# Three slots of an attention block's step reordered on TensorE, and a weight load moved forward in the load queue

## What is computed

```python
q = proj(query, Wk, bk); k = proj(key, Wk, bk); v = proj(values, Wv, bv)
scores = einsum("bhqd,bhkd->bhqk", q, k) / sqrt(dk)
p = softmax(where(allow, scores, NEG))
left = sum(p) - cumsum(p)
effect = clip(exp(-softplus(gamma) * sqrt(clip(left * |i - j|, 0))), 1e-5, 1e5)
attn = softmax(where(allow, scores * effect, NEG))
out = einsum("bhqk,bhkd->bhqd", attn, v)
x = layer_norm(query + concat(out) @ Wo.T + bo)
x = layer_norm(x + relu(x @ W1.T + b1) @ W2.T + b2)
```

## Time and profile before

| | us |
|---|---|
| median of 3 runs | 1475.06 |
| lowest and highest of the 3 runs | 1474.28, 1477.92 |
| the profiled execution, its own time | 1475.0 |
| span of that execution in the trace, first to last instruction | 1473.2 |
| TensorE busy | 1420.9 (96%) |
| VectorE busy | 1083.1 (74%) |
| ScalarE busy | 1026.9 (70%) |
| mean granted TensorE clock | 0.990 |

### The profile page before, as it was taken

How to read it: one execution, slowest core, us unless ns; L and a number is a source line. 1 busy time by engine, 2 the same in 40 slices (tenths; PEclk the granted TensorE clock), 3 DMA queues, 4 the chain that set the end, 5 groups by cost and what they waited for, 6 DMA issues and landing times.

```text
span 1473.2 us, 32758 instructions
## 1 busy us (share of the span) xinstructions
PE 1420.9 (96%) x12140; PEld 1154.5 (78%) x12140; DVE 1083.1 (74%) x3780; ACT 1026.9 (70%) x2626; POOL 155.2 (11%) x180
## 2 busy tenths in 40 slices
PE   5798899999999999999999999999999999999998
PEld 4455688888888888888888888888888888888787
DVE  6997868787887767786777868767786776777433
ACT  4775768777777768776677777668676776777522
POOL 4212010101001010000001010000100101000100
PEclk9999999999999999999999999999999999999999
DMA  8766667667576656656665655566656666666975
GB/s 286 275 237 223 248 216 267 230 245 254 199 291 217 239 205 248 211 200 241 231 239 196 256 209 208 223 220 236 234 203 227 220 227 217 248 229 229 329 292 188
DMA packets 89142, 345.90 MB, mean 235 GB/s; under 512 B 17624, under 2 KB 35800, under 8 KB 56344
## 3 DMA queue, kind: packets, MB, share of 16 engines
q1 hardware_dynamic: 76544, 335.06, 62.5%
q0 software_dynamic: 10208, 7.94, 1.8%
q10 hardware_dynamic: 2232, 0.81, 0.2%
HBM read 316.16 MB, written 27.53 MB: 233 GB/s over the span
## 4 chain that ended last, share of the span: by engine, by line
PE 91%; DVE 5%; DMA 1%; ACT 1%; issue 1%; SPq 0%; POOL 0%; ACTq 0%; DVEq 0%; POOLq 0%
PE bank L228 23%; PE bank L229 23%; PE bank L230 23%; PE bank L530 9%; PE bank L544 7%; PE bank L564 2%; PE bank L505 1%; PE bank L581 1%; PE bank L567 1%; DVE w_sb L1381 1%; DVE w_sb L1369 1%; DVE w_sb L1391 1%; DMA w_ring<-w_split 1%; DMA xc_raw<-x_t 0%; DMA zi_out<-z 0%
## 5 line engine op out<-in xcount | busy, mean ns | idle before, releaser
L228 PE MATMUL bank<-xt_hi,w_ring 128*128 128x256 f32 x1008 | 292.6, 290 | 8.5 <-DVE w_ring L1349 5.3
L229 PE MATMUL bank<-xt_lo,w_ring 128*128 128x256 f32 x1008 | 286.1, 284 | 0.0
L230 PE MATMUL bank<-xt_hi,w_ring 128*128 128x256 f32 x1008 | 285.9, 284 | 0.0
L965 ACT COPY pt_sb<-bank 128x512 f32<-128x512 f32 x192 | 111.2, 579 | 174.3 <-PE bank L544 171.8
L955 ACT ACTIVATE p_sb<-w_sb,nm 128x32 f32<-128x32 f32 (+7 forms) x512 | 205.3, 404 | 3.3 <-DVE nm L1396 3.3
L228 PEld LDWEIGHTS bank<-xt_hi,w_ring 128*128 128x128 f32 x1008 | 193.7, 192 | 14.6 <-issue 12.4
L228 PE MATMUL bank<-w_ring,h_hi 128*128 128x512 f32 x504 | 199.0, 395 | 0.9 <-DVE h_lo L1459 0.9
L229 PE MATMUL bank<-w_ring,h_hi 128*128 128x512 f32 x504 | 197.7, 392 | 0.0
L230 PE MATMUL bank<-w_ring,h_lo 128*128 128x512 f32 x504 | 197.2, 391 | 0.0
L229 PEld LDWEIGHTS bank<-xt_lo,w_ring 128*128 128x128 f32 x1008 | 194.0, 192 | 2.0
L230 PEld LDWEIGHTS bank<-xt_hi,w_ring 128*128 128x128 f32 x1008 | 193.9, 192 | 0.0
(11 more groups left out here) (144 smaller groups left out, 2613.0 us busy)
## 6 DMA issues: line engine op xcount, KB each, us to landing
w_ring<-w_split SPq DMA_DIRECT2D x248, 1024.0 KB, 5.1
w_split<-w_ring SPq DMA_DIRECT2D x32, 512.0 KB, 5.0
xc_raw<-x_t SPq DMA_DIRECT2D x16, 512.0 KB, 3.9
xc_raw<-ctx_t SPq DMA_DIRECT2D x16, 512.0 KB, 5.3
u_sb<-x_rows SPq DMA_DIRECT2D x16, 512.0 KB, 6.0
ring_raw<-w SPq DMA_DIRECT2D x32, 256.0 KB, 5.4
out<-rows SPq DMA_DIRECT2D x15, 512.0 KB, 7.0
zi_row<-zi_out POOLq DMA_DIRECT2D x58, 128.0 KB, 5.6
```

The source lines that it names most:

```text
L228: nc.tensor.matmul(dst, a_hi, b_hi, start=start, stop=False)
L229: nc.tensor.matmul(dst, a_hi, b_lo, start=False, stop=False)
L230: return nc.tensor.matmul(dst, a_lo, b_hi, start=False, stop=stop)
L965: nc.scalar.copy(pt_sb[:, n], pt_bank[:]).then_inc(pt_ok, 1)
```

## The change

On TensorE, three pairs of calls change places: in the first, second and fourth slot of `step`, the transposes now come first, then `attend`, then the scores. On SyncE, in the part for group 3 of `step`, the load behind the last pair of W2 (`w2_behind(i - 2, 7)`) and the last spare pair come after the load of `u_sb`, the load of `v_sb` and the load behind the first pair of W1 of the next batch (`w1_behind(i - 1, 0)`, which fetches that batch's third pair). Nothing is added or taken out, and `final()` on TensorE is not changed.

```diff
@@ SyncE, step, c == 3
                             sp.wait_ge(qk_mm, NQ * B)
                             spare_pair(5, 0)
-                        if ffn:
-                            w2_behind(i - 2, 7)
-                        if i == B:
-                            spare_pair(5, 1)
                         if last and now:
                             sp.wait_ge(x1_ok, RT * i)
                             sp.dma_start(u_sb[:], x_by_batch[i]).then_inc(xrow_in, 16)
...
                             v_load(i + 1)
                         if last:
                             w1_behind(i - 1, 0)
+                        if ffn:
+                            w2_behind(i - 2, 7)
+                        if i == B:
+                            spare_pair(5, 1)
+                        if last:
                             w1_behind(i - 1, 1)
                             w2_behind(i - 1, 0)
@@ TensorE, step
                 if last:
+                    transposes(i - 1, 2, 0)
                     attend(i - 1, 1)
-                if last:
-                    transposes(i - 1, 2, 0)
                 if now:
                     scores(i, 0, 0)
...
                 if last:
+                    transposes(i - 1, 3, 0)
                     attend(i - 1, 2)
-                if last:
-                    transposes(i - 1, 3, 0)
                 if now:
                     scores(i, 1, 0)
...
                 if now:
+                    transposes(i, 1, 0)
                     attend(i, 0)
-                    transposes(i, 1, 0)
                     scores(i, 3, 0)
```

## The result

| | us |
|---|---|
| changed kernel, median of 7 runs (lowest, highest) | 1467.3 (1465.55, 1472.02) |
| kernel before, median of 7 runs on the same chip (lowest, highest) | 1477.48 (1474.28, 1478.38) |
| ratio, 95% interval | 0.995 (0.9936 to 0.9963) |
| profiled execution of the changed kernel, its span | 1467.3, 1465.5 |
| forecast | 1466.9 (1464.4 to 1471.0), ratio 0.9945 |

The change is faster by 0.5%, as forecast. The single executions of the changed kernel spread by 6.5 us: the two medians differ by 10.2 us, the ratio stands for 7.4, and the two profiled executions differ by 7.7. So what each part brought is read from the traces, where the stretch that holds the slots repeats within 0.5 us.

What follows compares the result with a forecast made beforehand. TensorE was taken as the bound, busy 1420.9 of 1473.2 us. Slots 4.2, fourth slot 0 and load 3.9 sum to 8.1 us off 1475.0, giving 1466.9, range 1464.4 to 1471.0.

Steps and rivals of the forecast that it cites:

- A slot is worth 0.15 us: First and second slots of step: full matmul to scores falls from 1.70 to 1.55 us; 28 times, 4.2 us.
- the one place in the prologue: Behind turn_rows, eight transposes then an attend, 0.96 us; used to price four transposes to attend at 0.53.
- The fourth slot gives nothing: Fourth slot, 14 steps: 0.15 us saved each, waited again at transposes(i, 1, 1); gain 0.
- Its bound of 2.1 us: Rival: the fourth slot pays 14 x 0.15 us if the copy does not hold TensorE; 1464.8 us, chance 0.09.
- the hold: Fourth slot: TensorE waits at transposes(i, 1, 1) for ScalarE's copy, which ends 0.14 us before they start.
- The load lands 2.4 us sooner and the clock holds: Third W1 pair, before final: hidden(14, 2) starts 2.4 us earlier, clock 1.00 saves 1.5; 3.9 us together.
- the 0.3 us of stall that I expected to be left: Ahead of hidden(14, 2): weights wanted at 1367.79, block starting at 1368.1, instead of a 2.78 us stall.
- The sign that I had named: At the end: wait on w_ring<-w_split at most 0.5 us, hidden(14, 2) some 3 us at clock 1.00.
- What is late next: Near the end: the W2 pair, landing near 1370.5 for add_hidden(14, 1) near 1371.4, covered by 0.9 us.
- The clock in the fourth slot: Rival: 0.15 us longer wait at transposes(i, 1, 1) lowers the clock in 14 steps; 1487.6 us, chance 0.03.
- The sum was 8.1 us: Whole kernel: 4.2 from first and second slots, 0 from the fourth, 3.9 from the load; chance 0.62.

Runs made afterwards that it cites:

- e2: Kernel before with only the three reordered slots on TensorE, old load order; 1472.43 us, ratio 0.9979.
- e4: Changed kernel with the fourth slot back in its old order; 1469.03 us, ratio 0.9948.
- e7: Changed kernel with the spare load into wk_hi issued one step later, beside its partner; 1469.05 us, ratio 0.9945.
- e8: Changed kernel with project_rows' wait for the fourth feature group moved 9 matmuls later; 1469.49 us, ratio 0.9947.
- e10: Changed kernel, unaltered, measured again on the same chip; 1468.7 us, ratio 0.9934.
- e3: Kernel before with only the fourth slot reordered; 1477.59 us, ratio 1.0007.
- e5: Changed kernel with add_hidden(i - 2, 6) put ahead of transposes(i, 1, 1), and ScalarE's turned(i, 1, 1) behind effect's logarithm; 1460.61 us, ratio 0.9897.
- e6: Kernel of e5 with the fourth slot in its old order; 1463.48 us, ratio 0.9911.
- e1: Kernel before with only the SyncE load reordering, slots in old order; 1473.12 us, ratio 0.9976.

## Why the prediction was right, point by point

- **A slot is worth 0.15 us.** Right. 1.54 us against 1.55; transposes to attend took 0.53, as read from the one place in the prologue, and attend to scores 0.78. 26 slots gave 3.8 to 4.2 us in six executions (e2, e4, e7, e8, e10 and the changed one lie between 1153.20 and 1153.66), 0.145 to 0.163 each. The Trainium skill (TensorEngine Tiling (Array Packing), Key Properties) says that a change of tiling mode drains TensorE. An estimate with the length that its page TensorE: Matmul & The Clock Gate (Step-by-step) gives, about 128 cycles, is 0.05 us, a third of the 0.15 measured here.
- **The fourth slot gives nothing.** Right, and shown three ways: e3, e4, and e5 against e6. Its bound of 2.1 us was the value that it has without the hold.
- **The load lands 2.4 us sooner and the clock holds.** Right in kind and in the landing (1363.6; 1368.0 less the 4.6 us by which all came earlier is 1363.4). The stretch lost 3.66 us where 3.9 were forecast, and 4.1 to 4.3 in e1, e4 and e10: the 0.3 us of stall that I expected to be left was 0.6 in this trace, 0.1 in e4 and nothing in e1 and e10. The sign that I had named, a wait of at most 0.5 us, was missed by 0.1. `hidden(14, 2)` ran at a granted clock of 1.00 behind it.
- **What is late next.** The step that was missed. I named the W2 pair behind, with 0.9 us to spare, and it held. But `project_rows(15, 0)` came late by 0.5 us. Its input is made from VectorE's concat, which waited 3.30 us for the load of totals:

```profile
1392.80 0.65 DVE L1408 TENSOR_TENSOR cc_sb<-bank,zi_row 128x256 f32<-128x256 f32 x1 [3.30 <-DMA zi_row<-zi_out]
```

This load was issued at 1384.04 and took 8.7 us; in the kernel before it was issued at 1392.12 and took 7.3 (KB, us to landing; before, then after):

```profile
zi_row<-zi_out POOLq DMA_DIRECT2D x1, 128.0 KB, 7.3
zi_row<-zi_out POOLq DMA_DIRECT2D x1, 128.0 KB, 8.7
```

In the kernel before, what `project_rows` needs was there 1.1 us ahead of it. TensorE and the issue both came some 8 us earlier, so the longer landing made it late. The load took 8.5 to 9.1 us in the four executions that have the wait (the changed kernel, e1, e4, e6), and 5.1 to 7.6 in the eight that do not, among them all three with the old order of loads (before, e2, e3). So the wait comes from this landing. That the landing takes longer because the loads now stand closer together is my reading, not shown: with the same order it took 7.0 in e5 and 7.3 in e10. In the prediction's sum this is a term at nothing, where the profiled execution gave 0.6 us back.
- **The clock in the fourth slot.** The longer wait, 0.15 us more in each of 14 steps, let no clock fall: e3, which has it on its own, is as long as before in the second column, and its granted clock from 197 to 1350 us is 1.00, as before.

The sum was 8.1 us. The table's 4.24 + 3.66 - 0.60 = 7.3 is the change's. The 0.39 ahead of `hidden(0, 5)`, where the other two of the 28 slots lie (0.3 by the forecast), says nothing, as executions differ there by up to 4.5 us. The mechanism held, but that the median came within 0.4 us of the forecast is luck: single executions of the changed kernel lie between 1465.55 and 1472.02, and the forecast was counted from 1475.06, where the median of seven runs of the kernel before is 1477.48.

## What to carry to other kernels

Where an engine changes the shape of its work, count the changes and price one from start to start in the trace; here putting the transposes beside other 128 by 128 matmuls saves 0.15 us each time. Before such a gain is added up, look for the next point at which that engine waits for another: a gain ahead of it is given back there, and the same edit pays as soon as other work is put into the wait. Where a stall goes, follow every input of the blocks behind it, the small loads of other queues too, not only the next load in the same queue.

## What the runs showed of the hardware that I had not expected

The executions differ by up to 4.5 us before the steady part begins (`hidden(0, 5)` at 197.06 to 201.57 us), and by 0.5 us over the 1153 us behind in the six with the new first two slots and the wait for the copy. The stretch from 60 to 143 us of the changed kernel and of e8, with the granted clock behind the busy times:

```profile
60.00:143.00 83.00, 73.71 (x577) 44.93 (x570) 70.25 (x216) 53.83 (x142) 21.71 (x15) 0.94 0.72 259
```

```profile
60.00:143.00 83.00, 72.14 (x517) 43.26 (x510) 68.24 (x196) 50.55 (x129) 21.66 (x15) 0.90 0.68 244
```

In this stretch TensorE still waits often, and the execution of e8, which starts `hidden(0, 5)` 3.8 us later, was granted 0.90 of the clock instead of 0.94. The other executions go the same way but for one: all six with 0.90 here start `hidden(0, 5)` between 200.23 and 201.57 us, five with 0.94 or 0.96 between 197.06 and 198.15, and e4 has 0.94 and starts at 200.20. Whether the clock causes the difference, or both follow from something else, was not tested. For a change of 0.3% it means that one execution's span says little, and that one stretch of two traces says much.
